# The last attention tiles spread over the first 13 feed-forward steps, down weights turned behind the first up products, and a third residual buffer

## The reference

```python
qkv = x @ w_qkv.T                        # 256 q, 256 k, 512 v; 8 heads
q, k = xpos(q, k)
out = (q @ k.T * scale * decay_mask) @ v # causal, per head
y = silu(x @ w_gated.T) * head_norm(out) @ w_proj.T
x1 = layernorm(x + y)
h = silu(fp4(x1) @ fp4(w_gate).T) * (fp4(x1) @ fp4(w_up).T)   # 704 wide
result = layernorm(x1 + fp4(h) @ fp4(w_down).T)
```

## Time and profile before

| | |
|---|---|
| median of 3 runs | 631.68 us (630.91 to 632.49) |
| profiled execution, its own time | 630.28 us |
| its span in the profile | 628.3 us |
| busy share of the span: PE, DVE, ACT, POOL | 94%, 88%, 54%, 37% |
| granted TensorE clock, mean | 0.978 of full |

### The profile page before, as it was taken

One profiled execution on the slowest core, in us unless ns is written; L12 is line 12 of the kernel. 1 busy time (PEld: TensorE's weight loads), 2 busy tenths in 40 slices (PEclk: granted clock), 3 DMA queues, 4 the chain that ended last, 5 costly groups with the idle time before them and its releaser, 6 DMA issues.

```text
span 628.3 us, 14715 instructions
## 1 busy us (share of the span) xinstructions
PE 589.2 (94%) x4304; PEld 499.6 (80%) x4304; DVE 552.6 (88%) x1439; ACT 336.4 (54%) x869; POOL 231.9 (37%) x263
## 2 busy tenths in 40 slices
PE   7999999999999999999999696969999999999975
PEld 3788888887878787888878575868999888888864
DVE  6667899999999999999998757879999999999996
ACT  3356575666667675756666553424444444444433
POOL 2111223442343244234421205445444545444530
PEclk9999999999999999999999989788999999999998
DMA  6510111011001101110110000000000000000001
GB/s 208 198 44 14 47 53 42 8 50 50 26 24 50 50 11 40 50 42 8 50 33 17 9 8 2 2 0 18 17 17 17 28 22 17 17 17 17 17 18 51
DMA packets 24951, 22.10 MB, mean 35 GB/s; under 512 B 2009, under 2 KB 21858, under 8 KB 24930
## 3 DMA queue, kind: packets, MB, share of 16 engines
q1 hardware_dynamic: 24114, 20.27, 10.6%
q10 hardware_dynamic: 816, 1.57, 0.7%
HBM read 17.63 MB, written 4.20 MB: 35 GB/s over the span
## 4 chain that ended last, share of the span: by engine, by line
DVE 23%; issue 12%; POOL 8%; PE 4%; ACT 2%; DVEq 1%; ACTq 0%; POOLq 0%
POOL shared L1166 4%; POOL shared L1171 3%; DVE shared L801 3%; DVE shared L806 2%; DVE h_amax L786 2%; DVE shared L1001 2%; DVE shared L997 1%; DVE win_lo L918 1%; ACT shared L541 1%; PE wide_banks L1195 1%; DVE stats L934 1%; DVE h_inv L797 1%; PE upd_y L1195 1%; DVE win_lo L921 1%; DVE h_scale L791 1%
## 5 line engine op out<-in xcount | busy, mean ns | idle before, releaser
L1171 POOL TENSOR_TENSOR shared<-shared,h_scale 128x704 f32<-128x704 bf16 x32 | 44.5, 1391 | 92.0 <-DVE shared L806 92.0
L1195 PE MATMUL wide_banks<-wgu_hi,xq_hi 128*128 128x512 f32 (+1 forms) x192 | 63.6, 413 | 9.4 <-DVE xq_lo L990 9.4
L444 ACT ACTIVATE shared<-opened,rstd 128x64 f32<-128x64 f32 x256 | 64.6, 335 | 11.6 <-DVE rstd L719 11.2
L1195 PE MATMUL wide_banks<-win_hi,x_hi 128*128 128x512 f32 x192 | 67.6, 433 | 1.9 <-DVE shared L629 1.9
L415 ACT ACTIVATE shared<-shared 128x704 bf16<-128x704 f32 x32 | 25.3, 792 | 82.0 <-POOL shared L1166 82.0
L1258 PEld LDWEIGHTS mixed<-shared 128*128 128x128 f32 x512 | 62.0, 192 | 2.8
L1166 POOL TENSOR_TENSOR shared<-shared,h_inv 128x704 f32<-128x704 f32 x32 | 44.6, 1393 | 49.8 <-DVE h_inv L797 49.8
L1258 PE MATMUL mixed<-shared 128*128 128x64 f32 x512 | 60.6, 271 | 0.0
L1195 PE MATMUL wide_banks<-win_hi,x_lo 128*128 128x512 f32 x192 | 60.4, 396 | 0.0
L1195 PE MATMUL wide_banks<-win_lo,x_hi 128*128 128x512 f32 x192 | 60.3, 395 | 0.0
L1195 PE MATMUL wide_banks<-wgu_hi,xq_lo 128*128 128x512 f32 (+1 forms) x192 | 58.2, 385 | 0.0
(11 more groups left out here) (153 smaller groups left out, 1499.9 us busy)
## 6 DMA issues: line engine op xcount, KB each, us to landing
xf<-in_x_feat SPq DMA_DIRECT2D x32, 128.0 KB, 2.2
tab<-in_tables SPq DMA_DIRECT2D x16, 256.0 KB, 2.7
xt<-in_x_tok SPq DMA_DIRECT2D x32, 128.0 KB, 2.1
out<-shared SPq DMA_DIRECT2D x32, 128.0 KB, 1.7
x<-in_w_in ACTq DMA_DIRECT2D x3, 512.0 KB, 5.3
w<-in_w_gu SPq DMA_DIRECT2D x1, 1408.0 KB, 7.5
w<-in_w_down SPq DMA_DIRECT2D x1, 704.0 KB, 8.7
wgu_lo<-pow_dram SPq DMA_DIRECT2D x1, 576.0 KB, 4.5
```

What stands on the lines that cost most here:

```text
L444: last = act.activation(gated[:, b, cols], opened[:, b, cols], ACT.Copy, scale=rstd[:, b, 1 + k:2 + k])
L1171: pool.tensor_tensor(over_blocks(hq[:, b]), over_blocks(h_steps[:, b]), spread(h_fp4["scale"][:, b]), ALU.mult).then_inc(h_fp4["ready"], 1)
L1195: last = pe.matmul(dst, lhs, rhs, start=k == 0, stop=k == len(parts) - 1)
```

## The change

`finish(n)` keeps little: round 32's joint chain and `norm_x1`, `copy_gatedT` and `split_gated` of tile 29, and the PE parts. The rest stands in a new `left_over(n)`, called at the end of `ffn_body(n)` on DVE (after `h_round`) and ahead of `size_h` on ACT, in pieces for n = 0 to 13. `copy_gatedT` and `split_gated` of tiles 30 and 31 stand inside steps 1 and 2. `round_x1` stands at the end of POOL's steps 1, 9 and 13, where it was ahead of steps 2 and 6. To hold the pieces, FFN steps up to 13 are written out, and the loop runs from 14.

The three down groups are turned in the banks of `score`, one ahead of each of steps 0, 1 and 2. `gate_up(0)` waits for six groups and `turn_h(0)` for all nine. Tile 31's residual goes to a third buffer, and tile 30's projection to `mixed`.

```diff
+FFN_FROM = 7
...
-        W_PARTS = [range(0, 3), range(3, 5), range(5, W_GROUPS)]
+        W_PARTS = [range(0, 3), range(3, 5), range(5, len(GU_GROUPS))]
...
-            for n in range(first):
+            for n in range(2 * FFN_FROM):
                 finish(n)
                 ffn_body(n, n % 2)
-            finish(first)
-            with eng.Fori(LOOP_FROM, LOOP_TO) as i:
+            with eng.Fori(FFN_FROM, LOOP_TO) as i:
                 for b in range(2):
                     ffn_body(2 * i + b, b)
...
+
+        def turned_in(group):
+
+            return proj[:, group % 3] if group < len(GU_GROUPS) else score[:, group % 2]
+
+        def resid_of(n, b):
+
+            return resid[:, 2 if isinstance(n, int) and n == TILES - 1 else b]
+
+        def y_of(n):
+
...
+                if isinstance(n, int):
+                    left_over(n)
                 if valid(n - 1):
                     size_h(n - 1, 1 - b)
+                if isinstance(n, int) and n in (1, 2):
+                    copy_gatedT(TILES - LAG + n)
...
+            def left_over(n):
+                if n == 0:
+                    normalise_heads(TILES - 2, 0)
+                elif n == 1:
+                    normalise_heads(TILES - 1, 1)
+                    round_x_from(TILES)
+                elif n == 7:
+                    norm_x1(TILES + 2)
+                elif n == 9:
+                    round_x_from(TILES + 2)
+                elif n == 11:
+                    norm_x1(TILES + 4)
+                elif n == 13:
+                    round_x_from(TILES + 4)
...
-                need(dve, x1_ready, n - 1)
-                dve.tensor_tensor(resid[:, b], y, xt[:, b], ALU.add).then_inc(resid_done, 1)
+                if not (isinstance(n, int) and n == TILES - 1):
+                    need(dve, x1_ready, n - 1)
+                dve.tensor_tensor(resid_of(n, b), y_of(n), xt[:, b], ALU.add).then_inc(resid_done, 1)
...
+                if isinstance(n, int) and n in (1, 2):
+                    split_gated(TILES - LAG + n)
...
                 joint_root(n)
                 joint_shift(n)
 
-            def quantise_x(n):
-                x_scale(n)
-                x_inverse(n)
-                x_unit(n)
-                x_exponent(n)
+            def left_over(n):
+                if n == 0:
+                    turn_weights(len(GU_GROUPS))
+                    x_max(TILES)
+                    x_scale(TILES)
+                    x_inverse(TILES)
+                    x_unit(TILES)
+                    x_exponent(TILES)
+                elif n in (1, 3):
+                    if n == 1:
+                        turn_weights(len(GU_GROUPS) + 1)
+                    m = TILES - 3 + n // 2
+                    add_resid(m, m % 2)
+                    resid_stats(m, m % 2)
+                    last_moments(m, m % 2)
+                elif n == 2:
+                    turn_weights(len(GU_GROUPS) + 2)
+                elif n == 4:
+                    add_resid(TILES - 1, 1)
+                    resid_stats(TILES - 1, 1)
+                elif n == 5:
+                    joint_first(TILES + 2)
+                elif n == 6:
+                    joint_last(TILES + 2)
+                elif n == 7:
+                    x_max(TILES + 2)
+                    x_scale(TILES + 2)
+                    x_inverse(TILES + 2)
+                elif n == 8:
+                    x_unit(TILES + 2)
+                    x_exponent(TILES + 2)
+                elif n == 9:
+                    last_moments(TILES - 1, 1)
+                    joint_first(TILES + 4)
+                elif n == 10:
+                    joint_last(TILES + 4)
+                elif n == 11:
+                    x_max(TILES + 4)
+                    x_scale(TILES + 4)
+                    x_inverse(TILES + 4)
+                elif n == 12:
+                    x_unit(TILES + 4)
+                    x_exponent(TILES + 4)
 
             def finish(n):
                 if n == 0:
                     joint_chain(TILES)
-                if n < LAG:
-                    split_gated(TILES - LAG + n)
-                if n in (1, 2, 5):
-                    m = {1: TILES - 3, 2: TILES - 2, 5: TILES - 1}[n]
-                    add_resid(m, m % 2)
-                    resid_stats(m, m % 2)
-                    last_moments(m, m % 2)
-                if n == 1:
-                    x_max(TILES)
-                    quantise_x(TILES)
-                elif n == 3:
-                    joint_chain(TILES + 2)
-                elif n == 5:
-                    x_max(TILES + 2)
-                    quantise_x(TILES + 2)
-                    joint_chain(TILES + 4)
-                elif n == 6:
-                    x_max(TILES + 4)
-                    quantise_x(TILES + 4)
+                    split_gated(TILES - LAG)
...
+                if isinstance(n, int) and n in (1, 9, 13):
+                    round_x1({1: TILES, 9: TILES + 2, 13: TILES + 4}[n])
...
-                need(pe, resid_done, n)
+                need(pe, resid_done, n - 1 if isinstance(n, int) and n >= TILES - 2 else n)
                 pe.wait_ge(state_summed, n + LAG + 1 if not isinstance(n, int) else min(n + LAG + 1, TILES - BATCH))
-                accumulate(y, [(t[:, P * c:P * (c + 1)], w[:, c]) for t, w in
...
+                need(pe, w_lo_ready, group - 2 if group < len(GU_GROUPS) else group - 1 if group == W_GROUPS - 1 else 0)
...
-                        pe.wait_ge(w_lo_ready, W_GROUPS)
+                        pe.wait_ge(w_lo_ready, len(GU_GROUPS))
...
+                if isinstance(n, int) and n == 0:
+                    pe.wait_ge(w_lo_ready, W_GROUPS)
...
-                if isinstance(n, int) and n <= LAG:
-                    pe.wait_ge(gatedT_lo_ready, TILES - LAG + n)
+                if isinstance(n, int) and n in (1, 3, 4):
+                    pe.wait_ge(gatedT_lo_ready, TILES - LAG + {1: 1, 3: 2, 4: 3}[n])
...
-                if isinstance(n, int) and n == 1:
-                    pe.wait_ge(resid_done, TILES)
+                if isinstance(n, int) and n < 2:
+                    pe.wait_ge(resid_done, TILES - 1 + n)
...
             def finish(n):
-                if 1 <= n <= LAG:
-                    project_out(TILES - LAG - 1 + n)
-                if n < LAG:
-                    turn_gated(TILES - LAG + n, (TILES - LAG + n) % 2)
+                if n < W_GROUPS - len(GU_GROUPS):
+                    turn_weights(len(GU_GROUPS) + n)
+                if n in (1, 3, 4):
+                    project_out({1: TILES - 3, 3: TILES - 2, 4: TILES - 1}[n])
+                if n in (0, 2, 3):
+                    m = TILES - LAG + (n + 1) // 2
+                    turn_gated(m, m % 2)
```

More of the change, by code:

```diff
@@ L155, in retention_ffn @@
         wproj_lo = sb("wproj_lo", [P, VC, DM], F32R)
-        resid = sb("resid", [P, 2, DM])
+        resid = sb("resid", [P, 3, DM])
         x1 = sb("x1", [P, TILES, DM])
@@ L291, in weights @@
             return W_PARTS[part] if isinstance(n, int) and n == TILES - 1 else ()
+        def turned_in(group):
[3 more added lines that the diff above has]
+        def y_of(n):
+            return mixed[:, 0:DM] if isinstance(n, int) and n == TILES - 2 else y
         def resid2_of(n, b):
@@ L450, in norm_x1 @@
                     if valid(t):
-                        act.activation(x1[:, t], resid[:, 1 - row], ACT.Identity, bias=shift[:, row], scale=rstd[:, row, 0:1]).then_inc(x1_ready, 1)
+                        act.activation(x1[:, t], resid_of(t, 1 - row), ACT.Identity, bias=shift[:, row], scale=rstd[:, row, 0:1]).then_inc(x1_ready, 1)
             def place_state(n, b):
@@ L1056, in ffn_body, with joint_first @@
                     h_round(n - 1, 1 - b)
+                if isinstance(n, int):
+                    left_over(n)
             def joint_chain(n):
+                joint_first(n)
+                joint_last(n)
+            def joint_first(n):
                 joint_var(n)
@@ L1063, in joint_chain, with joint_last @@
                 joint_fine(n)
+            def joint_last(n):
                 joint_fine_square(n)
@@ L1179, in ffn_body @@
                     rescale_h(n - 1, 1 - b)
+                if isinstance(n, int) and n in (1, 9, 13):
+                    round_x1({1: TILES, 9: TILES + 2, 13: TILES + 4}[n])
             def finish(n):
[L1182 to L1186, removed]
+                pass
             both_loops(pool, body, ffn_body, finish)
@@ L1288, in project_out @@
                     pe.wait_ge(wproj_lo_ready, 1)
-                need(pe, resid_done, n)
+                need(pe, resid_done, n - 1 if isinstance(n, int) and n >= TILES - 2 else n)
                 pe.wait_ge(state_summed, n + LAG + 1 if not isinstance(n, int) else min(n + LAG + 1, TILES - BATCH))
-                accumulate(y, [(t[:, P * c:P * (c + 1)], w[:, c]) for t, w in
+                accumulate(y_of(n), [(t[:, P * c:P * (c + 1)], w[:, c]) for t, w in
```

(4 more changed lines are left out.)

28 lines of the change are left out of this document (9 added, 19 removed).

## The result

The changed kernel took 638.29 us as the median of four executions: 636.76, 637.20, 639.37 and one of 1130.89. The last was disturbed and is left out of the comparison, and the median of the other three is 637.20. The kernel before, four executions, has a median of 631.99. The ratio is 1.009, with a 95% interval from 1.0063 to 1.0116: the change costs 0.9%, which is 5.7 us, with 4.0 to 7.3 inside the interval. The forecast was 637.2, in a range from 629.5 to 640.5.

The account below looks back on a forecast made before the run. DVE's order was taken to bound the kernel: early part worth nothing, late pieces 18.8 us against 13.2 before, net +5.5 with 0.1 for moments, so 637.2 us against the median. Range 629.5 to 640.5 us.

Parts of the forecast that it names:

- Early part: Steps 0 to 4: new DVE waits of 9.8 us replace 9.4, so worth nothing, with 2 us either way.
- What a piece costs: Steps 5 to 14: pieces directly behind `h_round` are held by POOL's `rescale_h`; 18.8 us, where the work cost 13.2 before.
- Step 9: Tile 31's moments and `joint_first(36)`, beside POOL's `rescale_h` and `round_x1(34)`: 3.6 us extra DVE time.
- the upper case: Step 9's dependent chain is held again by each of POOL's instructions: 4.5 us, against 2.4 otherwise.
- Step 14: POOL's `round_x1(36)` holds `h_scale` and the norm chain's first instruction: 0.7 us.
- Steps 6, 8, 10 and 12: `joint_last` in 6 and 10, 2.3 us each; `x_unit` and `x_exponent` in 8 and 12, 2.1 and 1.8.
- Steps 7, 11 and 13: `x_max`, scale and inverse in 7 and 11, 2.0 and 1.9 us extra; no piece in 13, 0.
- The sum: Whole kernel: late pieces net +5.5 us, early part nothing, 637.2 us against the median; step 14 at about 484.
- the fast rival: Steps 5 to 12: pieces mostly not held by POOL, 4.9 us less than before, 626.8 us; 15%.
- Pieces slip past POOL: Steps 5 to 12: holds over eight pieces sum to under 4.9 us, 0.6 each, giving 626.8 us; 15%.
- No change: Early part gains 2 us, step 9 costs 2.4, POOL's delay in steps 8 and 12 doesn't show: about 633.4 us; 15%.
- Slower still: `turn_h(0)`'s wait and PE idling in steps 5 to 12 keep PE's clock low, two such steps: 641 us; 12%.

Follow-up runs that it names:

- e1_early_only: Changed kernel's steps 0 to 4 kept, rounds 34 and 36 again whole chains in `finish`; 632.24 us, ratio 0.9999 to the kernel before.
- e4_behind_max: Changed kernel with DVE's pieces of steps 5 to 12 moved behind the next step's `add_out` and `h_max`; 630.01 us, ratio 0.9973 to the kernel before.
- e6_fills: e4_behind_max with the three down groups' splits moved into DVE's waits in steps 0, 1 and 2; 626.51 us, ratio 0.991 to the kernel before.
- e7_dve_round: e4_behind_max with `round_x1` moved from POOL to DVE, ahead of `h_shift` in steps 1, 9 and 13; 628.09 us, ratio 0.9936 to the kernel before.
- e8_both: The edits of e6_fills and e7_dve_round together; 624.28 us, ratio 0.9876 to the kernel before.
- e3_mid_step: Changed kernel with DVE's pieces of steps 5 to 12 moved ahead of `h_shift`, where POOL idles; 630.89 us, ratio 0.9985 to the kernel before.

## Why the prediction was right

**Early part: right, and for the reason given.** `gate_up(0)` was forecast at about 358.6 and came at 358.86, DVE's waits at 9.8 and came to 10.2, `turn_h(0)`'s wait at 2.7 and came to 2.77 with the clock at half behind it, and step 5 at 401.9 and came at 402.63. Within the sum of waits the terms were off both ways: 1.93 for `xq_hi(1)` where 1.3 was taken, 0.68 for silu where 1.4 was, and 2.44 in step 3 where 1.8 was. e1_early_only has no difference in the total. The part is less certain than it looks: e4_behind_max has the same code up to step 4 and 8.7 us of waits, so an execution moves it by a microsecond or so. That the clock falls because of `turn_h(0)`'s wait isn't shown, as it is at 0.52 in e6_fills without the wait. That new waits took the old one's place is shown a second time by e6_fills, which puts work into three of them and gains 3.5 us.

**What a piece costs: right in mechanism and in the sum, less so in the terms.** The sum is 18.87 against 18.8, but that close only by luck, because errors of both signs met:
- *Step 9*, taken at 3.6 between 2.4 and 4.5, came at 4.33: the upper case. The forecast reasoned from two independent instructions at a seam of POOL's. A chain of dependent links behaves otherwise: each link issues once POOL's next instruction has begun, and so each of three was held.
- *Step 14*, taken at 0.7, came at 1.61. I counted `round_x1(36)`, and its two holds came as sized (`h_scale` 0.57 for 0.19, the next link of the norm chain 0.38 for 0.10, together 0.66), but not `h_to_unit`, which POOL runs right behind it (488.89) and which holds the link after that, 1.31 us at 488.99.
- *Steps 6, 8, 10 and 12*, taken at 2.3, 2.1, 2.3 and 1.8, came 0.4 to 0.6 lower. The pieces themselves last about what was forecast (from 439.32 to 441.46 in step 8, 2.14). Part of what was missed is the seam: a piece starts 0.08 ahead of the end of `h_round`, where `add_out` stands 0.10 behind it at the end of the loop's even steps. The rest is a credit: a loop step with the norm chain has a wait of its own for POOL's `rescale_h`, ahead of `h_scale`, and behind a piece POOL has long been done. `h_scale` of step 8 of after, at 433.21, doesn't wait. The same instruction in the trace of before, step 8, does:

```profile
437.78 0.19 DVE L791 TENSOR_SCALAR h_scale<-h_amax 128x44 f32<-128x44 f32 x1 [0.23 <-POOL shared L1171]
```

- Steps 7, 11 and 13 came 0.1 to 0.2 higher.
- Which link is held was off too: `poly` and not one of the first two in `joint_last`, the square and not `guess` in step 5. The price is about the same, since the hold ends with POOL's instruction whichever link it meets.

The Trainium skill (page SBUF — State Buffer, section Who interferes with whom) has the lock work in both directions, the first to issue blocking the second. The trace agrees: POOL's 1.70 at 439.54, behind `x_unit` (439.32 to 440.00), is 0.31 longer than its 1.39 elsewhere, and the 1.24 of a 2-element instruction behind POOL's start at 411.79 is the other direction. In step 12, where `x_unit` has half the width, POOL's instruction takes 1.44.

**The sum.** The pieces cost 18.87 where the same work cost 13.2 before, and another 0.3 in steps 5 and 6 of before that the forecast's 13.2 leaves out: +5.4, against +5.5. The early part, measured by the same rule, is 0.56 later (402.63 against 405.30 - 3.23 = 402.07). Step 15 so starts 2.61 + 5.92 = 8.53 us later (495.41 against 486.88), and stays so in the loop (509.68 against 501.15). Step 14 starts at 485.75 - 2.61 = 483.14, against the 484 that was forecast.

The forecast took it that from step 14 on all runs as before. There it failed, as near the end of the kernel another 0.67 is lost: the steps from 601.44 take 8.06 and 6.79 us, where those of before, from 592.96, take 7.70 and 6.48. In the first DVE waits 0.47 us ahead of `shift` (at 608.59). In the second `rescale_h` starts 0.31 later behind `h_round`, and `h_scale`, which ends with it, takes 0.66 where it took 0.34. All the kernels here but before, e7_dve_round and e8_both have this loss. The runs don't say what brings it.

The traces thus differ by 5.4 + 0.6 + 0.7 = 6.6 us, leaving out the 2.61, and the ratio says 5.7. Both lie in the interval. That the forecast's 637.2 is also the median of the three executions is in part luck. (The lower end of its range was to be half of the fast rival's way, which is 629.2 by its own numbers and not 629.5.)

**The rivals.** *Pieces slip past POOL* failed: it needed holds of under 4.9 us in all, 0.6 each. The held instructions took 0.8 to 1.1 us more than when free, and the three of step 9 3.1 more together, about 10 us in all. *No change* failed by all three of its terms: the early part gave nothing, step 9 was the upper case, and POOL's delay showed, by 0.31 us in step 8 though by only 0.05 in step 12. *Slower still* failed too: PE's clock in steps 5 to 13 is 0.98 where it was 0.93 in before's window. PE waits up to 3.62 us for `xq_lo` (at 454.92), and the clock of that step, 10, is 0.83, but in each of the other steps it is 1.00. In steps 5 and 6 DVE waits for nothing, and from step 7 to 14 PE waits for DVE's `xq_lo` in every step, so PE's own step never became the bound.

## What to carry to other kernels

A short chain on VectorE is priced by what GpSimd does at that moment: the pieces of steps 5, 6 and 9 add 1.00, 0.64 and 1.37 us to their step where GpSimd idles (e3_mid_step, in which GpSimd's instructions then hold step 10 instead). At the start of a 1.4 us GpSimd instruction the first two cost 2.06 and 1.75, and the third, beside three such instructions in a row, 4.33. So look for the place in the step where GpSimd idles, or where reductions and sums out of PSUM cover its instruction, and put the links there; here that alone turned +0.9% into -0.3%. Where a change takes one stall away, walk on to the next waits before counting a gain, and then put the loose work into those waits.

## What the hardware showed that was not expected

- A dependent chain is held again by every one of GpSimd's instructions that follow each other: 1.24, 1.21 and 1.18 us in step 9, with one free link of 0.16 ahead of the last.
- The hold ends with GpSimd's instruction, so work that isn't held shortens it: behind `x_max` at 0.68, `x_scale` took 0.94, and behind step 11's `x_max` at 0.41 it took 1.20.
- The two instructions of `round_x1` (512 columns) take 0.69 each on VectorE and 1.29 and 1.27 on GpSimd. Moving this work to the engine that bounds the kernel made steps 5 to 14 faster by 1.4 us and the kernel by 1.9.
